# Moving one VectorE subtraction ahead of a base product, and making SyncE wait for the spread blocks before a store and a load

## The reference

```
x = x + attn(layernorm(x))      # q, k, v, alpha, beta, gate from x; k is normalised
    S = S @ (a_t * (I - b_t * k_t k_t^T)) + b_t * v_t k_t^T      # 128 x 128 state, one step per position
    o_t = (q_t @ S) * g_t;  y = o @ Wo + bo
x = x + ffn(layernorm(x))       # rms norm, logits against 1024 slots, softmax over positions (dispatch)
    slots -> gelu(slots @ w1) @ w2 -> softmax over slots (combine) -> back to the positions
```

## Time and profile before

| what | value |
|---|---|
| median of three runs | 1288.08 us |
| time of the profiled execution | 1285.57 us |
| its span | 1283.7 us |
| TensorE (PE) busy | 1173.1 us, 91% |
| VectorE (DVE) busy | 904.5 us, 70% |
| ScalarE (ACT) busy | 727.2 us, 57% |
| GpSimd (POOL) busy | 241.0 us, 19% |
| share of the chain that ended last: DMA / SyncE's queue | 8% / 5% |

### The profile page before, as it was taken

One profiled execution on the slowest core, in us unless ns is written; L12 is line 12 of the kernel. 1 busy time (PEld: TensorE's weight loads), 2 busy tenths in 40 slices (PEclk: granted clock), 3 DMA queues, 4 the chain that ended last, 5 costly groups with the idle time before them and its releaser, 6 DMA issues.

```text
span 1283.7 us, 26857 instructions
## 1 busy us (share of the span) xinstructions
PE 1173.1 (91%) x8600; PEld 896.8 (70%) x8600; DVE 904.5 (70%) x2131; ACT 727.2 (57%) x1369; POOL 241.0 (19%) x275
## 2 busy tenths in 40 slices
PE   3599898899899978999999999999999999999999
PEld 2377677777777766467788467788467788466788
DVE  4567687788787774997445998445998445997444
ACT  3445555555555624577554477654478654477654
POOL 3355445565545540000000000000000000000000
PEclk9789999999999987999999999999999999999999
DMA  5113322223322124330212030212030212000012
GB/s 177 35 35 97 83 71 66 67 75 88 99 70 66 51 72 99 89 72 17 59 54 70 1 66 15 60 54 70 1 66 13 62 50 74 8 2 1 1 50 74
DMA packets 122044, 73.09 MB, mean 57 GB/s; under 512 B 50048, under 2 KB 119680, under 8 KB 121984
## 3 DMA queue, kind: packets, MB, share of 16 engines
q1 hardware_dynamic: 120656, 71.74, 20.7%
q10 hardware_dynamic: 1264, 0.53, 0.2%
q0 software_dynamic: 64, 0.00, 0.0%
HBM read 38.16 MB, written 25.69 MB: 50 GB/s over the span
## 4 chain that ended last, share of the span: by engine, by line
PE 52%; DVE 14%; issue 10%; DMA 8%; ACT 5%; SPq 5%; DVEq 1%; POOL 0%; ACTq 0%; POOLq 0%
PE m_wide L1874 13%; DMA Mrep<-M_dram 7%; PE m_wide L1852 7%; PE m_wide L1838 6%; PE m_wide L1759 5%; SPq L285 5%; PE m_wide L1863 4%; DVE m_Dm L1482 3%; ACT m_Eh L1648 2%; DVE rmax L1460 2%; DVE cmax L1458 2%; PE m_wide L1812 2%; DVE m_El L1490 2%; PE a_bank L1151 2%; PE a_bank L1061 1%
## 5 line engine op out<-in xcount | busy, mean ns | idle before, releaser
L1812 PE MATMUL m_wide<-m_X,m_Eh 128*128 (+1 forms) x1024 | 172.4, 273 | 16.6 <-DVE m_El L1490 16.5
L1759 PE MATMUL m_wide<-seT,XT 128*128 128x512 f16 x672 | 147.3, 379 | 0.7 <-issue 0.7
L1874 PE MATMUL m_wide<-m_Ph,m_Th 128*128 128x257 f16 x512 | 140.4, 274 | 1.7 <-DVE m_Pl L1521 1.7
L1812 PE MATMUL m_wide<-m_X,m_El 128*128 128x257 f16 (+1 forms) x512 | 139.7, 273 | 0.0
L1874 PE MATMUL m_wide<-m_Ph,m_Tl 128*128 128x257 f16 x512 | 139.4, 272 | 0.0
L1874 PE MATMUL m_wide<-m_Pl,m_Th 128*128 128x257 f16 x512 | 139.1, 272 | 0.0
L1580 DVE TENSOR_TENSOR m_Tl<-m_wide,m_Th 128x1024 f16<-128x1024 f32 x64 | 78.4, 1225 | 71.1 <-ACT m_Th L1687 70.6
L1812 PEld LDWEIGHTS m_wide<-m_X,m_Eh 128*128 128x128 f16 x1024 | 97.7, 98 | 40.2 <-DVE m_El L1490 19.8
L1759 PEld LDWEIGHTS m_wide<-seT,XT 128*128 (+1 forms) x672 | 65.5, 98 | 78.0 <-ACT L L1621 1.7
L1687 ACT CAST m_Th<-m_wide 128x1024 f16<-128x1024 f32 x64 | 64.7, 1011 | 86.1 <-PE m_wide L1863 86.1
L1621 ACT COPY L<-m_wide 128x512 f32 (+1 forms) x112 | 65.4, 587 | 84.3 <-PE m_wide L1759 83.9
(11 more groups left out here) (187 smaller groups left out, 2631.7 us busy)
## 6 DMA issues: line engine op xcount, KB each, us to landing
L<-in_L_attn_x_dram SPq DMA_DIRECT2D x16, 512.0 KB, 7.5
Mrep<-M_dram SPq DMA_DIRECT2D x16, 512.0 KB
x_dram<-x SPq DMA_DIRECT2D x16, 512.0 KB, 7.2
m_X<-X_dram SPq DMA_DIRECT2D x128, 64.0 KB, 1.8
m_x1t<-x_dram SPq DMA_DIRECT2D x64, 128.0 KB, 2.1
out_dram<-m_o SPq DMA_DIRECT2D x64, 128.0 KB, 1.7
X_dram<-Xh SPq DMA_DIRECT2D x16, 256.0 KB, 2.3
X_dram<-Xl SPq DMA_DIRECT2D x16, 256.0 KB, 2.3
```

The costliest lines, as they stand in the source:

```text
L1759: last = pe.matmul(lg[t % 4], XT[:, sx * KD + k, bass.ds((4 * g + t) * P, P)], seT[:, ss, k, z * HS:(z + 1) * HS], start=(c == 0), stop=(c ...
L1812: last = pe.matmul(acc[v][q], e[t % 4][:, qs], X[:, sx, bass.ds(4 * g + t, 1), 0:XW].rearrange("q a n -> q (a n)"), start=first and e is E ...
L1874: last = pe.matmul(co[p], a[p][:, es], pp[:, e, 0:XW], start=(c == 0), stop=(c == 3 * NS - 1))
```

## The change

Two edits are made. SyncE gets a wait for the landing of the spread blocks of chunk i + 2, between their issue and the store of chunk i; it stands in the steps in which both exist (i from 0 to 13). VectorE's subtraction of the last doubling is taken from behind the first `column` of the next step and put at the end of its own step, which is ahead of the first `product` of the next step.

```diff
+            def blocks_landed(c):
+
+                sp.wait_ge(Mrep_in, 16 * (c + 1))
+
             def store_x1(c):
...
                 if live(i + 2):
                     blocks_in(i + 2)
+                if live(i) and live(i + 2):
+                    blocks_landed(i + 2)
                 if live(i):
                     store_x1(i)
                 if live(i + 4) and live(i + 2):
...
                     if live(i + 2):
                         column(i + 2, s)
-                    if s == 0:
-                        if live(i + 1):
-                            doubling(i + 1, r, 2)
...
                 if live(i + 4):
                     biases(i + 4, q, 0)
+                if live(i + 2):
+                    doubling(i + 2, q, 2)
```

## The result

The changed kernel took 1304.11 us in the median of four runs (1297.47 to 1309.36), against 1288.17 us (1285.20 to 1289.89) before; the ratio is 1.0138, with a 95% interval from 1.011 to 1.0166. It is slower by 1.4%, some 16 us by the medians and 18 us by the ratio, where 8.4 us were forecast. The profiled execution took 1309.36 us, with a span of 1307.6 us; it is the slowest of the four, so what follows shows more of the loss than the median has.

A forecast was written before the change was run, and what follows sets the result against it. The chain repeated every chunk, 27.25 us from `M` through the spread blocks to the next `M`, was taken as the bound. Terms of +12, -1.5 and -2.1 us gave +8.4, 1296.5 us; 8 in 10: 1281 to 1307.

The forecast's parts named there:

- its last sentence: On TensorE: a changed granted clock in some turns was left out of the forecast, with no size given.
- the sum: Whole kernel: 12 late turns +12 us, three turns with the subtraction's gain -1.5, 14 faster block landings -2.1; net +8.4 us.
- The load's time: SyncE's load of x: usable 5.5 us after the store's issue, 5.7 after the first product's start (P), 1.15 late.
- From the statistics to PT: VectorE, statistics in front of `PT`: `PT` is late by the same 1.15 us as the statistics.
- heads: TensorE behind `PT`: starts 1.0 us late (0.55 to 1.7), the 1.15 us lateness less 0.15 us of slack.
- The blocks' landing: Spread-block DMAs, no longer sharing with store and load: 0.15 us gained a turn, between 0 and 0.6.
- The move: VectorE's 0.41 us subtraction moved into the wait for the blocks: a turn gains 0.5 us, bounds 0 and 1.06.
- the first rival: Load of x arrives in time, within 3.9 us of the store's issue: 1278 us, or 1272; chance 0.22.
- the second: Gains and a little lateness cancel, x usable 4.6 us from the store's issue: 1288 us; chance 0.18.
- the third: Load of x still takes its 7.5 us, 3.9 us late: +45 us, 1331 us; chance 0.04.

The follow-up runs named there:

- the move alone: Kernel before with only the last doubling's subtraction moved, no wait on SyncE: 1279.26 us, ratio 0.995.
- the wait alone: Kernel before with only SyncE's wait added, the subtraction left where it was: 1295.63 us, ratio 1.0082.
- the pairs of the table: Kernel before with VectorE's statistics of x moved behind `PT`, plus neither edit (ratio 0.9965), the moved subtraction (0.9928), SyncE's wait (0.9921) or both (0.9891).

## Why the prediction was right or wrong

The direction and the main mechanism held: the wait makes the load late, the statistics stand in front of `PT`, `PT` in front of `heads`, and `heads` sets the next `M`. The size was less than half of what came. The step of the prediction that failed is its last sentence, "A changed granted clock of TensorE in some turns is not in the sum": it put at nothing, without a reason, what the turns at half clock cost. 10.8 us of the profile belong there, and filling TensorE's gap took 9 us of the loss back. The rest of the sum came out near its 8.4 us (11.3 at full clock), but by luck, since three of its terms were off in both directions.

- *The load's time.* I had x usable 5.5 us after the store's issue (5.05 to 6.2), P + 5.7. Store and load were issued at P + 0.17 and P + 0.90, and the statistics started at P + 5.24 in the turn shown; that is 5.07 us. In the mean of the 12 turns it is 5.21 (4.96 to 5.44), near the lower end. That leaves 0 to 0.4 us for the slow start of a load behind a store, where I had added 0 to 0.7.
- *From the statistics to PT.* I took the 1.40 us of before. It was 2.20 us in the mean, for the collision with GpSimd that the shift brought about. A term I did not have, 0.8 us a turn.
- *heads.* Forecast 1.0 us later against P; measured P + 8.15 to 8.46 in the full-clock turns against 6.80 to 6.95 before, some 1.45 us. That is the two misses together, and a third: of the 0.15 us between `PT`'s end and `heads` I took 0.10 for slack with the move and all of it with the wait, but from `PT`'s start to `heads`' it is 0.83 us in both kernels and with the move alone, so there was none.
- *The blocks' landing.* Taken at 0.15 us, measured 0.7 (7.39 to 6.71 from issue to P in the wait alone) and 0.5 to 0.6 in the pairs of the table. I read the fastest turn beside both transfers as a sign that sharing is free. The sum at full clock came out at +0.94 us a turn where I had +0.85, but by errors of both signs.
- *The move.* Taken at 0.5 us a turn, measured 0.38 alone, of which `PT` has 0.2. An operation of 0.41 us was counted by its duration; but it started at 298.02, the next product 0.33 us later, and without it that product starts earlier by less, since it has to wait for the column before it anyway:

```profile
297.88 0.22 DVE L580 TENSOR_TENSOR Zc<-a_const,tmp 128x60 f32<-128x60 f32 x1
...
298.35 0.20 DVE L569 TENSOR_TENSOR tmp<-Mrep,Zc 128x56 f32<-128x56 f32 x1
```

  That product starts at P + 0.73 here and at P + 0.52 with the move alone, 0.2 us earlier. With the statistics out of the way of `PT`, the move was worth nothing that the turns show.
- *The rivals.* The load was never usable in time for the first rival, which asked for 3.9 us from the store's issue; its turn of 26.6 to 26.8 us came only when the order on VectorE was changed. Nor was it as early as the 4.6 us of the second or as late as the third had it. By the fixed cost and the rate that the Trainium skill ("DMA: Bandwidth & Descriptors", Anatomy of one DMA) has for one DMA of GpSimd's path, the estimate for both transfers was 4.4 us; on SyncE's queue the traces don't agree, with 5.21.

## What to carry to other kernels

A wait put on a queue's issuer moves everything behind it on that queue: look for who uses the last of those transfers, and move that user to behind the work that others are waiting for before adding the wait; here this turned +1.4% into -1.1%. When work shifts in time, look at what runs on the other engines at the new place, and at how long TensorE will stand idle in one piece. If an idle stretch must be, put work that isn't urgent into it.

## What the runs showed of the hardware

- TensorE idle for some 1.9 us in one piece in front of `heads` came with half of the granted clock in 8 of 12 turns, in two profiles. With a 0.59 us gap at the same place and the same work in the turn it was in none of 12. In the wait alone it was in one, and that turn had 2.00 us in one piece in front of the matmuls of L1157; the other eleven, with two gaps of up to 1.19 and 1.66 us, kept their clock. Over all profiles it was 21 of 30 turns with 1.88 us or more in one piece, and none of 114 with 1.75 us or less.
- A VectorE operation of 0.17 us with both inputs in SBUF lasted up to 1.03 us beside GpSimd's product of 1.04 us over 512 columns, and 0.21 us beside one of 1.04 us over 4 columns.
- From the issue of the spread blocks (512 KB) to the first product it was 6.7 us in the mean with nothing behind them, 7.2 to 7.6 with the store and then the load, and 7.9 with the load alone close behind.
